# x, its second copy, the gate and the output laid out chunk by chunk in DRAM: 256 KB in one piece for 512 tokens

## What is computed

```
for n, layer in enumerate((L0, L1, L2, L3)):
    v = group_norm(x)                        # 32 groups of 2 channels, statistics over all tokens
    # L0, L1: layernorm, then left and right = projection * mask * sigmoid(projection)
    # L2:     a, b = sigmoid(product of two projections), 16 channels, no layernorm
    # L3:     layernorm, then a, b = sigmoid(projection) * projection
    k = einsum over one token axis (left, right)   # one 256x256x256 product per channel
    x = x + gate(v) * or before (layernorm(k) @ W_out)
return x
```

## Time and profile before

| | |
|---|---|
| median of the runs | 2094.15 us |
| the profiled execution's own time | 2098.47 us |
| its span | 2096.6 us |
| TensorE busy | 1779.0 us (85%) |
| ScalarE busy | 1372.8 us (65%) |
| VectorE busy | 1326.5 us (63%) |
| GpSimd busy | 1006.1 us (48%) |
| packets of the DMA queue, share of 16 engines | 68.4% |
| moved | 496.17 MB, mean 237 GB/s |

### The profile page before, as it was taken

One profiled execution on the slowest core, in us unless ns is written; L12 is line 12 of the kernel. 1 busy time (PEld: TensorE's weight loads), 2 busy tenths in 40 slices (PEclk: granted clock), 3 DMA queues, 4 the chain that ended last, 5 costly groups with the idle time before them and its releaser, 6 DMA issues. The chain is left out here.

```text
span 2096.6 us, 40996 instructions
## 1 busy us (share of the span) xinstructions
PE 1779.0 (85%) x10389; PEld 1041.3 (50%) x10389; DVE 1326.5 (63%) x2984; ACT 1372.8 (65%) x2541; POOL 1006.1 (48%) x916
## 2 busy tenths in 40 slices
PE   0899997797998899995599799789799999699776
PEld 0445454685554445453255477633344444588433
DVE  7566666124763677776977388466377778344675
ACT  0577876355996788874499666477577787344554
POOL 0267678003991577776699300089222223000599
PEclk9999999798999999998899899999899999899999
DMA  7357876774996355546399666089547777845599
GB/s 325 123 181 235 246 231 218 268 290 170 366 367 232 101 188 173 187 149 253 135 349 366 242 217 209 32 316 375 193 150 232 234 236 216 296 179 222 187 397 377
DMA packets 326949, 496.17 MB, mean 237 GB/s; under 512 B 22828, under 2 KB 188463, under 8 KB 320439
## 3 DMA queue, kind: packets, MB, share of 16 engines
q1 hardware_dynamic: 326838, 494.93, 68.4%
HBM read 285.12 MB, written 197.13 MB: 230 GB/s over the span
## 5 line engine op out<-in xcount | busy, mean ns | idle before, releaser
L804 POOL TENSOR_TENSOR lo<-xn,hi 128x512 f16<-128x512 f32 x192 | 224.0, 1167 | 374.1 <-DVE hi L736 230.6
L601 PE MATMUL ps<-w_heads,hi 64*128 64x256 f16 x3072 | 294.0, 274 | 10.2 <-DVE sig L750 4.5
L1112 ACT ACTIVATE O<-ps 128x512 f32 (+1 forms) x144 | 151.8, 1054 | 190.5 <-PE ps L1033 190.5
L750 DVE SCALAR_TENSOR_TENSOR sig<-ps,largest,sig 128x512 f32<-128x512 f32 x256 | 180.8, 746 | 142.8 <-ACT sig L664 141.9
L664 ACT ACTIVATE sig<-ps,largest 128x512 f32<-128x512 f32 x384 | 246.2, 692 | 30.7 <-PE ps L601 28.6
L645 ACT ACTIVATE zs<-ps,shift 128x512 f32<-128x512 f32 x192 | 131.9, 687 | 191.4 <-PE ps L569 188.5
L1349 POOL TENSOR_TENSOR shared<-O,out_rs 128x128 f32<-128x128 f32 (+1 forms) x112 | 76.4, 684 | 370.8 <-DVE out_rs L1249 369.8
L601 PEld LDWEIGHTS ps<-w_heads,hi 64*128 64x128 f16 x3072 | 153.9, 95 | 167.1 <-DVE sig L750 67.3
L1397 PEld LDWEIGHTS ps<-ident,shared 128*128 128x128 f32 (+1 forms) x1024 | 120.0, 133 | 225.5 <-issue 96.4
L1397 PE MATMUL ps<-ident,shared 128*128 128x128 f32 (+1 forms) x1024 | 160.8, 282 | 75.6 <-POOL shared L1349 48.9
L601 PE MATMUL ps<-w_heads,lo 64*128 64x256 f16 x1536 | 213.5, 273 | 0.0
(11 more groups left out here) (164 smaller groups left out, 3724.3 us busy)
## 6 DMA issues: line engine op xcount, KB each, us to landing
shared<-left_right SPq DMA_DIRECT2D x34, 2048.0 KB, 12.0
shared<-gate SPq DMA_DIRECT2D x224, 256.0 KB, 4.6
gate<-gates SPq DMA_DIRECT2D x96, 512.0 KB, 2.9
x_dram<-shared SPq DMA_DIRECT2D x192, 256.0 KB, 4.3
shared<-x_dram SPq DMA_DIRECT2D x192, 256.0 KB, 4.7
xs<-x_dram SPq DMA_DIRECT2D x64, 512.0 KB, 4.2
left_right<-stage SPq DMA_DIRECT2D x64, 448.0 KB, 6.0
left_right<-shared SPq DMA_DIRECT2D x64, 448.0 KB, 5.7
```

The source lines that it names most:

```text
L601: last = pe.matmul(PAIR[row][:, g, kb * S:kb * S + S], tokens[half, q % 8, at:at + P], k["w_heads"][half, part, :], start=(step == 0), sto ...
L750: dve.scalar_tensor_tensor(dst, pair(row, 1), k["largest"][:, 1:2], factor, ALU.mult, ALU.mult).then_inc(pair_read.sem, 1)
L804: pool.tensor_tensor(lo[:, q % 8, :], xn[:, q % 2, :], hi[:, q % 8, :], ALU.subtract).then_inc(c["lo_done"].sem, 1)
L1112: act.activation(o_of(ch), ps[h % 4 // 2][:, h % 2, :].rearrange("p (b g i) -> p b g i", b=2, g=2), ACT.Copy).then_inc(c["o_copied"].sem, 1)
```

## The change

The five arrays are laid out [64 chunks, 128 partitions, 512 tokens]: a chunk is 256 KB in one piece, in which a partition has 2 KB, and the next chunk begins 256 KB further. The arrays are then viewed with the axes in the order partition, chunk, token, and each DMA takes one, two or four chunks of that view. The tiles in SBUF are what they were. The host's reordering of input and output changes with it.

For the DMAs this means:

- one chunk (all of `output` and `project_plain`): 128 pieces of 2 KB as before, but next to each other instead of 128 KB apart;
- two chunks (`project`, loads of x and stores of the gate): 256 pieces of 2 KB instead of 128 of 4 KB;
- four chunks (first statistics): 512 pieces of 2 KB instead of 128 of 8 KB.

No DMA is added, removed or moved, and no instruction of a compute engine differs: every engine has the same instructions in the same order with the same waits. What differs in an instruction is the address pattern of the DMAs. The arrays of `left_right` stay as they are.

```
-                    sp.dma_start(xin[:, s, :], x[:, bass.ds((t * 4 + s) * wide, wide)]).then_inc(c[f"xc_in{s}"].sem, 16)
+                    sp.dma_start(xin[:, s].rearrange("p (m e) -> p m e", e=CH), x[:, bass.ds((t * 4 + s) * 4, 4), :]).then_inc(c[f"xc_in{s}"].sem, 16)
...
-                sp.dma_start(xs[:, q % 8:q % 8 + 2, :].rearrange("p a b -> p (a b)"),
-                             x[:, bass.ds(m * CH, 2 * CH)]).then_inc(c[f"x_in{q % 8 // 2}"].sem, 16)
+                sp.dma_start(xs[:, q % 8:q % 8 + 2, :], x[:, bass.ds(m, 2), :]).then_inc(c[f"x_in{q % 8 // 2}"].sem, 16)
...
-                sp.dma_start(gate[:, bass.ds(m * CH, 2 * CH)],
-                             gates[:, q % 4:q % 4 + 2, :].rearrange("p a b -> p (a b)")).then_inc(c[f"gate_out{q % 4 // 2}"].sem, 16)
+                sp.dma_start(gate[:, bass.ds(m, 2), :], gates[:, q % 4:q % 4 + 2, :]).then_inc(c[f"gate_out{q % 4 // 2}"].sem, 16)
...
-                sp.dma_start(xs[:, q % 8, :], x[:, bass.ds(m * CH, CH)]).then_inc(c[f"x_in{q % 8}"].sem, 16)
+                sp.dma_start(xs[:, q % 8, :], x[:, bass.ds(m, 1), :].rearrange("p m e -> p (m e)")).then_inc(c[f"x_in{q % 8}"].sem, 16)
...
-                sp.dma_start(x_new[:, bass.ds(m * CH, CH)], xo[:, q % RING, :]).then_inc(c[f"x_out{q % RING}"].sem, 16)
+                sp.dma_start(x_new[:, bass.ds(m, 1), :].rearrange("p m e -> p (m e)"), xo[:, q % RING, :]).then_inc(c[f"x_out{q % RING}"].sem, 16)
...
-        out[name] = nc.dram_tensor(name, [P, HALF * S], F32, kind="Internal").ap()
+        out[name] = nc.dram_tensor(name, [NCH, P, CH], F32, kind="Internal").ap().rearrange("m p e -> p m e")
```

More of the change, by code:

```diff
@@ L858, in store @@
                 sp.wait_ge(c["gate_done"].sem, c["gate_done"](m + 1))
-                sp.dma_start(gate[:, bass.ds(m * CH, CH)], gates[:, q // 2 % 4, :]).then_inc(c[f"gate_out{q // 2 % 4}"].sem, 16)
+                sp.dma_start(gate[:, bass.ds(m, 1), :].rearrange("p m e -> p (m e)"), gates[:, q // 2 % 4, :]).then_inc(c[f"gate_out{q // 2 % 4}"].sem, 16)
             for q in range(6):
@@ L1194, in load_x @@
                 sp.wait_ge(free.sem, free(m - 3))
-                sp.dma_start(xs[:, q % RING, :], x[:, bass.ds(m * CH, CH)]).then_inc(c[f"xc_in{q % RING}"].sem, 16)
+                sp.dma_start(xs[:, q % RING, :], x[:, bass.ds(m, 1), :].rearrange("p m e -> p (m e)")).then_inc(c[f"xc_in{q % RING}"].sem, 16)
             def load_g(i, q):
@@ L1203, in load_g @@
                 slot = q // EVERY % RING
-                sp.dma_start(gs[:, slot, :], gate[:, bass.ds(m * CH, CH)]).then_inc(c[f"gc_in{slot}"].sem, 16)
+                sp.dma_start(gs[:, slot, :], gate[:, bass.ds(m, 1), :].rearrange("p m e -> p (m e)")).then_inc(c[f"gc_in{slot}"].sem, 16)
             def step(i, q, more):
@@ L1557, in layouts @@
     x = v["x"].reshape(2, HALF * S, C).transpose(0, 2, 1).reshape(P, HALF * S)
-    arrays = {"x": x}
+    arrays = {"x": x.reshape(P, NCH, CH).transpose(1, 0, 2)}
     arrays.update(constants())
@@ L1628 @@
     a.update(scratch(nc))
-    out = nc.dram_tensor("out", [P, HALF * S], F32, kind="ExternalOutput").ap()
-    build(nc, a, out)
+    out = nc.dram_tensor("out", [NCH, P, CH], F32, kind="ExternalOutput").ap()
+    a["x"] = a["x"].rearrange("m p e -> p m e")
+    build(nc, a, out.rearrange("m p e -> p m e"))
     r = run_bass_kernel_spmd(nc, [{f"in_{name}": v for name, v in arrays.items()}], core_ids=[0])
     y = np.asarray(r.results[0]["out"])
+    y = y.transpose(1, 0, 2)
     return y.reshape(2, C, HALF * S).transpose(0, 2, 1).reshape(1, S, S, C)
```

## The result

The change makes the kernel slower, by little: 2098.41 us (median of 12 runs, 2091.82 to 2107.99) against 2093.05 us of the kernel before in the same comparison (12 runs, 2088.69 to 2095.32). The ratio is 1.0029, 95% interval 1.0016 to 1.0042. A second series gave 2103.11 against 2093.06 us, ratio 1.0044 (1.0027 to 1.006). The forecast was 2095.8 us and "same" by the prediction's bound of 4.2 us. The medians differ by 5.4 us (10.0 in the second series), the ratios give 6.1 and 9.2 us. The loss is clear of nothing; the first interval begins at 3.3 us, so that it does not exclude the 4.2 us.

The account below looks back on a forecast made before the run. No single limit: DMA and VectorE bound the first statistics, TensorE the projections and L0's and L1's outputs, GpSimd L3's output. Terms +2.8 + 0.3 - 1.5 = +1.6 us on 2094.15 gave 2095.8 us, range 2088 to 2101.

Parts of the forecast that it names:

- the prediction's bound of 4.2 us: Whole kernel: 0.2% of the predicted median, about what a measurement can tell from no change; "same" had chance 0.53.
- the sum: Whole kernel: +2.8 + 0.3 - 1.5 = +1.6 us, giving a predicted median of 2095.8 us.
- the second rival: First statistics: 2 KB reads reach only 369 GB/s, VectorE waits every tile; +6.0 us, 2100.2 us, chance 0.20.
- Bounds: By stage: first statistics fill DMA and VectorE; TensorE paces L0's and L1's outputs, which stay at 365 to 369 GB/s.
- Part 1: First statistics: loads cut from 8 KB to 2 KB pieces, 396 GB/s for 424; +2.8 us, between 0 and +5.7.
- The first landing: First statistics: the first load of xin arrives 0.2 us later at 396 instead of 424 GB/s.
- The rival with 369 GB/s: First statistics bind harder: 2 KB reads no faster than L1's output; +6.0 us, decided from 381 GB/s, chance 0.20.
- Part 2: Projections of L0, L1, L3: pieces cut from 4 KB to 2 KB, hidden under TensorE; +0.3 us, between 0 and +0.7.
- the first loads of three blocks: Projections: TensorE's waits of 4.0 and 2.1 us were put here; the only extra on the path, 3 x 0.1 = +0.3 us.
- Part 3: Outputs and L2's projection: same 2 KB pieces, now adjacent; -1.5 us, between 10.1 us gained and 7.4 us lost.
- The harder first stage: First statistics: 2 KB reads at 369 GB/s, nothing gained in the outputs; +6.0 us, 2100.2 us, chance 0.20.
- Relief: L2 and L3: separate pieces ease memory and the transfers' waits go; -7.0 us in all, 2087.2 us, chance 0.27.

Follow-up runs that it names:

- e2: Kernel before with padded xin slots, so first-statistics loads go in 2 KB pieces at the old addresses: 2100.41 us, ratio 1.003 to the kernel before.
- f4: Changed kernel with 64 one-chunk loads instead of 16 four-chunk loads in the first statistics: 2106.6 us, ratio 1.0057 to the kernel before.
- f2: Kernel before with xs and gates padded in project, so two-chunk transfers move 2 KB pieces: 2094.93 us, ratio 1.0006 to the kernel before.
- f3: Changed kernel with x alone partition by partition as before; copies, gate and output chunk by chunk: 2100.2 us, ratio 1.0027 to the kernel before.
- f1: The kernel before run again without an edit, for a second profile: 2094.19 us, ratio 0.9998 to the kernel before.
- g3: Changed kernel with x partition by partition as before and x loaded 16 chunks ahead instead of 14: 2088.44 us, ratio 0.9982 to the kernel before.
- g2: Kernel before with x loaded 16 chunks ahead instead of 14: 2086.56 us, ratio 0.9973 to the kernel before.
- e3: Changed kernel with x alone laid out by four chunks, [16, 128, 2048]: 2102.76 us, ratio 1.0037 to the kernel before.
- e4: Kernel before with x, both copies and the gate laid out by four chunks, the output as before: 2130.59 us, ratio 1.0177 to the kernel before.
- e1: The changed kernel run again without an edit, for a second profile: 2103.11 us, ratio 1.0044 to the kernel before.

## Why the prediction was right in its range and wrong in its parts

**The time.** 2098.41 us lies in the range 2088 to 2101 and the kernel moved the way that the sum said, but by 5.4 us for 1.6, and the second series' 2103.11 us is above the range. The range took the time in because it had been drawn around the second rival, and the misses below all go one way.

**Bounds.** Right: the first statistics were full on both sides and lost; the outputs of L0 and L1 did not move at all.

**Part 1** was the right mechanism with the wrong size. The term was +2.8 us and measured +4.0, within its bounds. The rate was taken as 396 GB/s and is 387: 15.73 MB take 40.6 us for 37.1, +3.5. That is e2's 393 GB/s for the size of the piece, close to the 396 that I took from L3's output, and something more that came with the new addresses and that I had not priced. The time of a packet, worked out as in the prediction, is 2048 x 16 x 1.05 / 387 = 89 ns; of the two prices there, 87 was near, and 92 was itself a slip for 91 (2048 x 16 x 1.02 / 369). The first landing was put at +0.2 us and is +0.6, of which e2 shows 0.1 for the piece's size. By the Trainium skill ("DMA: Bandwidth & Descriptors", section "Why small descriptors are slow (HBM only)") the rate would have been an estimated 410 GB/s. No run here reads 2 KB pieces that fast: even e2, which changes nothing but the piece, stays at 393. The rival with 369 GB/s had said that 381 was the point of decision; f4 comes near it with 384.

**Part 2** holds the step that was wrong as a reading: "Loads are 14 chunks ahead. TensorE hides it." I counted only the extra queue time (224 ns for a transfer at most), and f2 bears that out: 1.0006, nothing to be seen. But the lead that counts is from the load to its first reader, which is 12 chunks ahead itself, not to the chunk at hand. The two steps between, 6.1 us in the change's timeline, are less than the 8.1 us that the load takes to land beside the `left_right` stores, and TensorE already waited there before the change: the 4.0 and 2.1 us of the earlier trace rows, which I put down to the first loads of three blocks. Their count says otherwise, 5 and 5 times. Taking the waits away gave back 5.7 us of the kernel before, and f3's distance to it went from 5.7 to 1.9 us. It did not make the change as a whole cheaper (6.7 us), so this step does not account for what the sum lacks.

**Part 3** was put at -1.5 us, and nothing of it is shown. The 372 GB/s of L2's output are not bound to the layout (f1, the same kernel, has 381), g3 is not faster than g2, and e2, with the old addresses in this stage, is 2.05 us shorter there than the first profile too. GpSimd's waits for stores fell from 10.1 to 7.5 us, but f1 has 5.6 + 2.1 = 7.7 without any change. The bounds held.

**The sum.** +4.0 for +2.8 in the first stage. Outside it, by the ratios, +2.1 us for -1.2 in the first series (6.1 - 4.0) and +5.2 in the second (9.2 - 4.0). The terms that missed are thus part 1's, 1.2 us too small, part 3's gain of 1.5, of which nothing is shown, and a loss of some 2 to 5 us outside the first stage where the sum had +0.3, and its cause stays open.

**The rivals.** The harder first stage (2100.2 us) was nearer to the measured time than the forecast, in sign and in most of its price, though by 387 and not 369 GB/s. Relief came nowhere. On the Trainium skill's rule on pitch ("DMA: Bandwidth & Descriptors", section "Latency and other measured facts") this case says: at a pitch of 128 KB, below all that it lists, there was nothing to win from contiguous tiles, since e3 and f3 read 424 GB/s with the one and with the other. The pitch that did harm was a small one, 8 KB between pieces of 2 KB in e4, which no row of before could show.

**Still open.** What in the chunk layout's addresses costs the 1.2 us of the first stage is not settled; f4 speaks against the 256 KB between a partition's pieces, or its 64 DMAs hide it. That the loads in `project` came later by the layout is not shown either: the sums of waits overlap (6.1 in before, 5.9 in e2, 5.8 in f3). In L1's projection, where only the loads of x and the stores of the gate differ, the loads take 4.36 or 4.37 us on average to land in before, f1 and e2, 4.50 in f2 and 4.46 to 4.58 in the change, e1, e3, f3 and f4: the cut to 2 KB pieces alone goes as far as the chunk layout, and f2 shows no loss by it. Of f3's 5.7 us, about 2 are left with the longer lead, some 1.6 go with its lower mean clock, and why that was lower in its runs was not tried. An axis order that keeps both the 8 KB pieces of the first stage and another pitch in the copies was not run with the lead of 16.

## What to carry to other kernels

Ask of a layout what every one of its readers gets as the contiguous piece: the tile of the most frequent DMA was made one piece here, and the reader that took four tiles at a time, with the queue full, lost 9% of its rate (424 to 387 GB/s). Measure a prefetch from its issue to its first reader, and look whether the engine waits there already; a lead of "14 chunks" was two steps, and two more gave 0.27%, as much as the whole change had cost. Where an effect is below 0.5%, profile the kernel before twice, and trust those stages alone that repeat. When a stage begins later in one kernel, move the window with it: e4's L3 output reads 317 GB/s from 1975 to 2090 us, where 20 us of the triangle are in it, and 364 in its own time. And to see whether a wait explains a loss, take it out of both kernels.

## What the runs showed of the hardware

- In the first statistics, with the queue full, loads in pieces of 8 KB went at 424 GB/s at a pitch of 128 KB and as one piece of 1 MB; pieces of 2 KB went at 393 GB/s one behind another, at 387 with 256 KB between a partition's pieces, and at 384 as single DMAs of 256 KB in one piece. An estimate from the first two windows (312 ns for 8 KB, 2048 x 16 x 1.05 / 393 = 87.5 ns for 2 KB): a packet costs about 13 ns beside what goes with its bytes.
- Pieces of 2 KB that lie 8 KB apart did 333 and 364 GB/s in the outputs of L2 and L3 (in L3's the loads alone lie so), where a pitch of 128 KB did 372 to 381 and 396 to 398.
- Issuing four stores of `left_right` held SyncE's queue for 4.06 us and the next four for 7.38 us in the change; f1 has 3.85 and 7.49, the first profile of before 3.84 and 8.07. A DMA written behind them is that much later, whatever its lead is called.
- Behind a wait of TensorE of 2.14 to 2.46 us at this place the granted clock was at 1.2 GHz for about 3.4 us, in five profiles of five; behind 0.34 to 1.56 us in none of five.
